# A graph layer on one core: dense edge weights computed by ScalarE in PSUM, and eight groups of edges gathered last

## What is computed

```python
hs, hd = h[src], h[dst]
e = concatenate([hs, hd], axis=1)
a_k = exp(relu(e @ W_att_k + b_att_k))            # k = 1, 2, 3, one number an edge
att_k = segment_sum(a_k, dst)
avg_a = (a_1 / att_1[dst] + a_2 / att_2[dst] + a_3 / att_3[dst]) / 3
m = avg_a * relu(relu(relu(hs @ W1 + b1) @ W2 + b2) @ W3 + b3)
h_neigh = segment_sum(m, dst) / maximum(deg, 1)
out = relu(concatenate([h, h_neigh], axis=1) @ W_c1 + b_c1) @ W_c2 + b_c2
return layernorm(x + out)
```

## Time and profile before

| | us |
|---|---|
| median of three runs (lowest, highest) | 785.11 (784.7, 786.55) |
| the profiled execution | 788.37 |
| its span in the profile | 784.4 |
| busy: TensorE, VectorE, GpSimd, ScalarE | 635.0, 562.6, 573.6, 460.2 |
| mean granted TensorE clock, share of full | 0.858 |

### The profile page before, as it was taken

How to read it: one execution, slowest core, us unless ns; L and a number is a source line. 1 busy time by engine, 2 the same in 40 slices (tenths; PEclk the granted TensorE clock), 3 DMA queues, 4 the chain that set the end, 5 groups by cost and what they waited for, 6 DMA issues and landing times.

```text
span 784.4 us, 17056 instructions
## 1 busy us (share of the span) xinstructions
PE 635.0 (81%) x5157; PEld 519.2 (66%) x5157; DVE 562.6 (72%) x1855; ACT 460.2 (59%) x1109; POOL 573.6 (73%) x604
## 2 busy tenths in 40 slices
PE   9951889988878777999998788797778877878775
PEld 5741657764655456899988677685667766767664
DVE  4884587588888787788886666665567777677566
ACT  6566687578655455667765555553365556566533
POOL 7777777777777677777777777777777777777760
PEclk9985596599778776899999989988798988899698
DMA  7974263334862233333433333324344444444321
GB/s 228 252 195 105 66 101 84 71 85 78 69 83 75 54 96 80 83 87 87 88 83 80 78 74 83 73 64 133 66 107 104 104 111 128 104 117 104 89 59 35
DMA packets 83313, 75.69 MB, mean 96 GB/s; under 512 B 35064, under 2 KB 66720, under 8 KB 83216
## 3 DMA queue, kind: packets, MB, share of 16 engines
q0 software_dynamic: 19008, 39.82, 25.8%
q1 hardware_dynamic: 63920, 34.59, 16.3%
q10 hardware_dynamic: 288, 0.13, 0.1%
HBM read 64.94 MB, written 9.52 MB: 95 GB/s over the span
## 4 chain that ended last, share of the span: by engine, by line
PE 33%; POOL 30%; issue 13%; DVE 11%; ACT 6%; DMA 5%; DVEq 1%; SPq 0%; POOLq 0%; ACTq 0%
POOL work L1247 30%; PE bank L1434 8%; PE bank L1473 7%; PE bank L1457 4%; PE bank L1440 2%; DVE counts L1730 2%; ACT fin L1578 2%; DVE acc L1907 2%; PE bank L592 2%; PE bank L613 2%; PE bank L1391 1%; DVE fin L1717 1%; PE bank L601 1%; DMA message_table<-work 1%; PE bank L1419 1%
## 5 line engine op out<-in xcount | busy, mean ns | idle before, releaser
L1247 POOL DMA_INDIRECT work<-message_table,src_t x554 | 531.6, 960 | 174.2 <-issue 164.9
L1434 PE MATMUL bank<-work 128*128 128x144 f32 (+8 forms) x1188 | 188.5, 314 | 37.9 <-DVE acc L1907 37.8
L1434 PEld LDWEIGHTS bank<-work 128*128 128x128 f32 x1188 | 174.3, 223 | 50.8 <-issue 43.8
L1604 ACT COPY work<-bank 128x192 f32<-128x192 f32 (+7 forms) x126 | 37.4, 297 | 177.4 <-DVE work L1859 176.0
L1473 PE MATMUL bank<-shared,fin 128*128 128x129 f32 (+1 forms) x882 | 115.1, 286 | 0.0
L1907 DVE TENSOR_TENSOR acc<-acc,bank 128x192 f32 (+8 forms) x297 | 89.1, 300 | 27.4 <-issue 3.6
L1473 PEld LDWEIGHTS bank<-shared,fin 128*128 128x128 f32 (+1 forms) x882 | 106.1, 197 | 2.5 <-issue 0.6
L1890 DVE TENSOR_TENSOR work<-bank,work 128x576 f32<-128x576 f32 (+7 forms) x126 | 86.2, 684 | 13.1
L1765 DVE SCALAR_TENSOR_TENSOR fin<-logits_or_x,per_node,counts 128x384 f32<-128x384 f32 (+1 forms) x147 | 85.8, 611 | 1.9 <-PE bank L1473 1.9
L904 PE MATMUL bank<-rest_w,acc 128*128 128x128 f32 x294 | 52.3, 344 | 40.5 <-DVE fin L995 31.0
L904 PEld LDWEIGHTS bank<-rest_w,acc 128*128 128x128 f32 x294 | 46.5, 246 | 43.0 <-DVE fin L995 32.3
(11 more groups left out here) (162 smaller groups left out, 840.4 us busy)
## 6 DMA issues: line engine op xcount, KB each, us to landing
work<-message_table,src_t POOLq DMA_INDIRECT x554
side<-near_nodes SPq DMA_DIRECT2D x102, 48.0 KB
side<-logit_parts SPq DMA_DIRECT2D x297, 0.8 KB
message_table<-work SPq DMA_DIRECT2D x12, 262.0 KB, 4.7
work<-message_table SPq DMA_DIRECT2D x48, 65.5 KB
work<-in_x_t SPq DMA_DIRECT2D x12, 256.0 KB, 4.9
fin<-in_x SPq DMA_DIRECT2D x11, 256.0 KB, 3.0
logits_or_x<-in_x_t SPq DMA_DIRECT2D x11, 256.0 KB, 3.7
```

Source lines behind the costliest of these rows:

```text
L1247: pool.indirect_dma_start(out=rows_of(n)[:, t, :], out_offset=None, in_=table[:, :], in_offset=bass.IndirectOffsetOnAxis(ap=src_t[:, h, g: ...
L1434: pe.matmul(sums[:, at:at + HEADS * w], rows_here[:, t, 0:P], wt_of(i)[:, t, :], start=h == 0, stop=h == TILES - 1)
```

## The change

Dense weights: `scale_rows` goes. ScalarE computes relu(A*B - 1) for a block and a head over 384 destinations into the bank `EXP_BANK` (`hot_excess`), and VectorE's `hot_weights` reads that bank, adds 1 (or 0 where a bound on the logits fails) and multiplies by the counts. TensorE takes the loaded rows unscaled. There is one bank: write `n` waits for weight `n - 1` (`s_hw`), weight `n` for write `n` (`s_hr`). ScalarE's order in a step is write 1, mask copy, exp, one-hots, write 2, write 0 of the next block. SyncE's reload of a block's buffer waits for the block's matmuls instead of its scaling.

Order: groups 100 to 107, whose edges end in node block 3, leave their place among the long units and become four short units at the end. There are 22 long units of four groups and 127 units in all. A bound on their nodes joins the check for the second pass.

Finals: block 3 becomes the last piece, alone. The others are three blocks, ten times four, two, two and one, so there are 15 pieces. `A`, `B` and `C` start nine, six and four steps before the end of the loop, and `final_tail` is written anew.

The diff, cut to its core (left out: assertions, buffer views, the lists of the late rows' transfers):

```diff
@@ -62,6 +62,7 @@
 EARLY_FROM, EARLY_EVERY = 3, 2
+LATE_BLOCK, LATE_FROM, LATE_GROUPS = HOT, 100, 8
@@ -125,13 +126,19 @@
     HOT_AT = COUNT_STEPS + 2
-    LONG = COUNT_STEPS
+    LONG = COUNT_STEPS - 1
     long_from = -(-n_hot // (2 * pair)) * 2 * pair
-    long_end = long_from + (LONG - 1) * 2 * pair
-    assert long_end < n_groups and CELL % (2 * pair) == 0
+    late_a, late_b = LATE_FROM, LATE_FROM + LATE_GROUPS
+    long_end = long_from + (LONG - 1) * 2 * pair + LATE_GROUPS
+    assert long_end < n_groups and CELL % (2 * pair) == 0 == (late_a - long_from) % (2 * pair)
+    assert long_from <= late_a and late_b <= long_end and late_a // CELL == (late_b - 1) // CELL
+    assert LATE_GROUPS % (2 * pair) == 0
     first_order = [tuple(range(n_hot, long_from))]
-    first_order += [tuple(range(g, g + 2 * pair)) for g in range(long_from, long_end, 2 * pair)]
+    first_order += [tuple(range(g, g + 2 * pair)) for g in range(long_from, long_end, 2 * pair)
+                    if not late_a <= g < late_b]
     first_order += [tuple(range(g, min(g + pair, n_groups))) for g in range(long_end, n_groups, pair)]
+    MAIN = len(first_order)
+    first_order += [tuple(range(g, g + pair)) for g in range(late_a, late_b, pair)]
     again_order = [tuple(range(g, min(g + pair, n_groups))) for g in range(0, n_groups, pair)]
@@ -255,8 +262,8 @@
         hot_wt = fin[:, 0:THREE * n_hot_w].rearrange("p (j k d) -> p j k d", j=THREE, k=HEADS)
-        shared = sb("shared", [P, TWO * HEADS * (P + 1)])
-        hot_scaled = shared[:, :].rearrange("p (j k f) -> p j k f", j=TWO, k=HEADS)
+        SHARED = 5 * P
+        shared = sb("shared", [P, SHARED])
         n_out = HOT * HEADS * (P + 1)
@@ -488,6 +495,8 @@
                 dve.memset(one_col[:, :], 1.0)
+                dve.memset(less_one[:, :], -1.0)
+                dve.memset(shared[:, COLS:SHARED], 0.0)
                 dve.memset(eps_col[:, :], EPS / DOWN)
@@ -666,35 +675,38 @@
-        sizes = [CHUNK] * (n_blocks // CHUNK - 1)
-        rest = n_blocks - sum(sizes) - 1
-        sizes += [rest - rest // 2, rest // 2, 1]
-        finals = [(sum(sizes[:c]), nb) for c, nb in enumerate(sizes)]
+        n_four = (n_blocks - LATE_BLOCK - 1) // CHUNK - 1
+        sizes = [LATE_BLOCK] + [CHUNK] * n_four
+        rest = n_blocks - 1 - sum(sizes)
+        sizes += [(rest - 1) // 2, rest // 2, 1]
+        finals = [(sum(sizes[:c]) + (c > 0), nb) for c, nb in enumerate(sizes)] + [(LATE_BLOCK, 1)]
         FINAL_EVERY, FINAL_STEPS = (4, 3), 8
         A, B, C = LAST - 3, LAST - 2, LAST - 1
+        assert sorted(i for b, nb in finals for i in range(b, b + nb)) == list(range(n_blocks))
         assert finals[LAST][1] == 1 and finals[B][1] <= LAST_FROM and finals[C][1] <= LAST_FROM
             most = share * n_edges + 6 * math.sqrt(share * (1 - share) * n_edges)
-            return min(len(first_order) - 1, sum(u[-1] < int(most / GROUP) for u in first_order))
+            return min(MAIN - 1, sum(u[-1] < int(most / GROUP) for u in first_order[:MAIN]))
             final_at.append(max(at_least, expected_end(c) + 2))
-        final_at += [expected_end(A) + 1, expected_end(B) + 1]
-        assert final_at[A - 1] + 3 <= final_at[A] == U - 9 and final_at[B] == U - 5 and expected_end(C) <= U - 3
-        ready = [at - 2 for at in final_at[:A]] + [expected_end(A), expected_end(B), expected_end(C), U - 1]
+        final_at += [U - 9, U - 6, U - 4]
+        assert final_at[A - 1] + 3 <= final_at[A] and U - 4 == MAIN
+        assert all(expected_end(c) < final_at[c] for c in (A, B, C))
+        ready = [at - 2 for at in final_at[:A]] + [at - 1 for at in final_at[A:]] + [U - 1]
         final_tail = {
-            U - 4: [(B, 1), (A, 5)],
-            U - 3: [(B, 2), (A, 6)],
-            U - 2: [(B, 3), (A, 7)],
-            U - 1: [(C, 0), (B, 4), (LAST, 0), (LAST, 1), (C, 1), (LAST, 2), (B, 5), (C, 2), (LAST, 3), (LAST, 4),
-                    (C, 3), (LAST, 5), (B, 6), (C, 4), (B, 7), (C, 5), (LAST, 6), (C, 6), (LAST, 7), (C, 7)],
+            U - 4: [(B, 2), (A, 5), (C, 0), (C, 1)],
+            U - 3: [(B, 3), (C, 2), (A, 6), (B, 4), (B, 5), (B, 6)],
+            U - 2: [(C, 3), (A, 7), (B, 7), (C, 4)],
+            U - 1: [(LAST, 0), (LAST, 1), (C, 5), (LAST, 2), (C, 6), (LAST, 3), (C, 7), (LAST, 4), (LAST, 5), (LAST, 6),
+                    (LAST, 7)],
         }
...
@@ -730,10 +742,12 @@
             for g in u:
-                node_limits[g] = least_node(i)
+                node_limits[g] = least_node(i) if i < MAIN else LATE_BLOCK * P
         limit_runs = [(a, len(list(run))) for a, run in itertools.groupby(node_limits)]
-        limit = mask[0:1, 1:THREE, :].rearrange("p j c -> p (j c)")[:, 0:n_groups]
-        assert n_groups <= (THREE - 1) * columns_most
+        n_limits = n_groups + LATE_GROUPS
+        limits = mask[0:1, 1:THREE, :].rearrange("p j c -> p (j c)")[:, 0:n_limits]
+        limit, late_limit = limits[:, 0:n_groups], limits[:, n_groups:n_limits]
+        assert n_limits <= (THREE - 1) * columns_most
@@ -1275,7 +1295,7 @@
                         if b >= BLOCKS:
-                            sp.wait_ge(s_hr, HEADS * (b - BLOCKS + 1))
+                            sp.wait_ge(s_hm, b - BLOCKS + 1)
                         m = block_nodes(b)
@@ -1466,14 +1486,14 @@
                                           zero_col[:, 0:1].to_broadcast([P, HEADS * (P + 1)]), start=True, stop=False)
-                        pe.wait_ge(s_hr, HEADS * (b + 1))
+                        rows_here = hot_block[0:m, b % BLOCKS, 0:1 + P]
+                        pe.wait_ge(s_hb[b % BLOCKS], 16 * (b // BLOCKS + 1))
                         for k in range(HEADS):
                                                  hot_wt[0:m, b % THREE, k, h * P:(h + 1) * P],
-                                                 hot_scaled[0:m, b % TWO, k, :],
-                                                 start=False, stop=b == n_blocks - 1 and k == HEADS - 1)
+                                                 rows_here, start=False, stop=b == n_blocks - 1 and k == HEADS - 1)
                         last.then_inc(s_hm, 1)
@@ -1530,18 +1550,17 @@
-                    def scale_rows(b):
-
-                        m = block_nodes(b)
-                        if b == 0:
+                    def hot_excess(b, k):
+
+                        m, n = block_nodes(b), HEADS * b + k
+                        if n == 0:
+                            act.wait_ge(s_hl, 16 * (HEADS * HOT + 1))
+                            act.wait_ge(s_cadd, n_hot)
                             act.wait_ge(s_ok, OK_STEPS)
-                            act.wait_ge(s_e3, EARLY)
-                        act.wait_ge(s_hb[b % BLOCKS], 16 * (b // BLOCKS + 1))
-                        if b >= TWO:
-                            act.wait_ge(s_hm, b - TWO + 1)
-                        for k in range(HEADS):
-                            act.activation(hot_scaled[0:m, b % TWO, k, :], hot_block[0:m, b % BLOCKS, 0:1 + P], ACT.Copy,
-                                           scale=powers[0:m, b, k:k + 1]).then_inc(s_hr, 1)
+                        else:
+                            act.wait_ge(s_hw, n)
+                        act.activation(bank[EXP_BANK][0:m, 0:hot_nodes], hot_b[0:m, k, :], ACT.Relu, bias=less_one[0:m, 0:1],
+                                       scale=powers[0:m, b, k:k + 1]).then_inc(s_hr, 1)
@@ -1632,6 +1651,8 @@
                     for i in range(n_steps):
+                        if first and 0 <= i - HOT_AT - 1 < n_blocks:
+                            hot_excess(i - HOT_AT - 1, 1)
                         if i + 1 < n_units:
@@ -1656,7 +1677,9 @@
                         if first and 0 <= i - HOT_AT - 1 < n_blocks:
-                            scale_rows(i - HOT_AT - 1)
+                            hot_excess(i - HOT_AT - 1, 2)
+                        if first and 0 <= i - HOT_AT < n_blocks:
+                            hot_excess(i - HOT_AT, 0)
@@ -1684,7 +1707,10 @@
                                                 ALU.is_lt))
-                        chain(dve.tensor_reduce(late[:, :], limit[0:1, :], AX, ALU.max))
+                        most_late = float((LATE_BLOCK + 1) * P - width_of(late_a))
+                        chain(dve.tensor_scalar(late_limit[0:1, :], bank[SIDE_BANKS[0]][0:1, late_a:late_b], most_late, None,
+                                                ALU.is_gt))
+                        chain(dve.tensor_reduce(late[:, :], limits[0:1, :], AX, ALU.max))
                     dve.wait_ge(s_fill, 1)
@@ -1756,14 +1782,11 @@
                         m = block_nodes(b)
-                        if b == 0 and k == 0:
-                            dve.wait_ge(s_hl, 16 * (HEADS * HOT + 1))
-                            dve.wait_ge(s_cadd, n_hot)
-                            dve.wait_ge(s_ok, OK_STEPS)
+                        dve.wait_ge(s_hr, HEADS * b + k + 1)
                         if b >= THREE:
```

(5 more changed lines are left out.)

33 lines of the change are left out of this document (19 added, 14 removed).

## The result

The changed kernel takes 813.94 us, median of six runs (811.19 to 819.67), against 783.71 us (781.25 to 786.55) of the kernel before in the same comparison: a ratio of 1.0394, interval 1.035 to 1.0437, or 30.2 us more. The forecast was 795 us in a range of 781 to 808. The direction was right, the size was not: 20.6 us are missing from a sum that came to +9.6.

A forecast was written before the change was run, and what follows sets the result against it. Gathers were taken to set the pace before, and the consumers after the change. Terms +6.2 (dense), +2.7 (unit), -2.3 (narrower units), +6 (finals) and -3 (tail) gave +9.6 on 785.1: 795 us, range 781 to 808.

The forecast's parts named there:

- The turn on the bank: Dense stage: ScalarE and VectorE alternate on one PSUM bank three times a block; mean step 5.18 us, stage 40.0 us longer.
- The lag isn't worked off to the end: After the dense stage: of its 40.0 us, +6.2 stays after later gather waits absorb what they can.
- the pace of units with finals: While finals run, a unit costs 4.57 us without gather waits, so a lead is worked off at only 0.4 us a unit.
- Of the 40.0 the later waits for gathers absorb at most their 33.8: Behind the dense stage: VectorE's 33.8 us of gather waits taken off the 40.0 us of longer stage.
- left: What remains of the dense stage's 40.0 us after the later gather waits absorb their share: +6.2 us.
- (4) Tail [...] -3: Behind the last addition: block 3 alone as last piece, 10.9 us instead of 13.6; with a narrower last unit, -3.
- Unit, finals and block 3: One more unit +2.7 us, narrower last units -2.3, finals +6 for three more blocks inside the loop and one more piece.
- Gathers the bound: Rival: gathers stay the bound, the lead being worked off before the last unit; 781 us, chance 0.17.
- partly: Rival: the lead is partly worked off, at 0.58 to 0.63 us a write; 782 to 790 us, chance 0.15.
- Ring full: Rival: steps over 5.45 us fill the 48-tile ring, so gathering stops too; 808 us, chance 0.08.
- The late block doesn't pay: Rival at the end: block 3's finals only replace the last blocks', losing the 3 us; 798 us, within the forecast's 0.60.

The follow-up runs named there:

- Kernel 3: The changed kernel with ScalarE's excess written to three SBUF buffers instead of the one PSUM bank, same instruction order: 784.53 us, ratio 1.0017.
- kernels 3 and 6: 6: dense change with three SBUF buffers, a block's three writes together a step ahead: 783.85 us in the old order, 787.15 us in the new.
- Kernel 1: The kernel before with only the dense weights changed; order, finals and end list as before: 800.19 us, ratio 1.0215.
- three lags: Units 30 to 77 longer by 28.0, 43.6 and 58.7 us: kernel before plus two zero matmuls a dense block, dense change alone, kernel before plus three.
- the pair with three matmuls: Three zero-adding matmuls per dense block but the last, added to the kernel before (816.86 us) and to the kernel with the new order alone (829.59 us).
- the old list: The whole change with the old end list: pieces B and C stay out of the last units and run behind the last unit; 803.84 us, ratio 1.0258.
- kernel 2: The kernel before with only the order, the finals' pieces and the end list changed; dense weights as before: 789.05 us, ratio 1.0088.
- two matmuls: The kernel before with two zero-adding matmuls added to each dense block but the last: 789.97 us, ratio 1.0106.

## Why the prediction was right and wrong

**The turn on the bank: right.** 675 ns for a write of 0.67 forecast, 614 for a weight of 0.61, 5.19 us for a step of 5.17 to 5.18. The stage grew by 41.7 us (252.2 less 210.5) where +40.0 was forecast, by 43.2 in the dense change alone. Kernel 3 shows that the turn is the cause. The prediction's case for 0.61 proved less than it said: it drew its 1.05 ns a column through the bank's 344 ns and SBUF's 611 ns, and then found the two on one line. A slope from other rows would have carried it, since L1890, which reads a bank, takes 608 ns for 432 columns and 758 for 576, 1.04 a column. A weight that reads the bank takes 614 ns, one from SBUF 611, and the same instruction in kernels 3 and 6, from SBUF, 613 and 611. The Trainium skill ("VectorE: DVE Perf Modes", section on the TRN2 errata) has 62 cycles more for PSUM, an estimated 0.065 us; the trace doesn't agree, the difference is 3 ns.

**The lag isn't worked off to the end: right,** and the pace of units with finals too. Kernel 1 took 170.0 us for 37 units from unit 80 to the ninth last, 4.59 us each; the forecast was 4.57. The changed kernel took 179.8 us for 38, 4.73 each.

**"Of the 40.0 the later waits for gathers absorb at most their 33.8": the first step that failed.** The bound was taken as the value. Over three lags the later stages gave back 21.8, 27.1 and 26.1 us. By stretch, the waits of before behind the dense stage are 6.1 us up to unit 80, 19.2 to the ninth last and 8.5 in the last eight (33.8 in all); kernel 1 recovered 7.2, 14.7 and 5.1. A wait for gathers had covered others that came out when it went: behind the dense stage VectorE waited 7.1 us for TensorE's logits (3.3 before) and 14.8 for ScalarE's exps (13.2 before), and TensorE's own waits for VectorE stayed. So the term "left" was 43.6 - 27.1 = 16.5 and not 6.2: 10.3 of the missing 20.6 us, some 3 in the stage and 7 in what was absorbed.

**"(4) Tail [...] -3": the second.** The tail did shrink, by 2.3 us in the traces. But the sum counted only what lies behind the last addition. The steps of `B` and `C` that left the tail had gone into the last units, at places where nothing covers them, and those units were priced by their narrower columns alone (-2.3). For last units and tail together the sum thus has -5.3 where the traces have +2.8 against the dense change alone, and +1.7 in the pair with three matmuls. With the old list the whole change costs 10.1 us less by the medians (the two ratios, 1.0394 and 1.0258 with their intervals, leave 6 to 15); the two traces place 7.1 us of it in the last eight units, less the 2.6 us of tail, 4.5 in all. The other 5.6 us I could not place: the two kernels were not timed together, from unit 29 to the ninth last their stages differ by 2.9 us the other way, and 10.3 of the 11.9 us between their spans lie before unit 29's sums, which the list doesn't touch.

**Unit, finals and block 3: of the right size.** Forecast +2.7 and +6 less 2.3, together 6.4 without the tail. The whole change with the old list less the dense change alone: 3.6 us by the medians. The traces have 9.7 us more in the second column of the changed kernel than in the dense change alone, against the +2.7 and +6.

**The step from 6.4 and -3 to 13.7.** By the medians: 16.5 for the turn, 3.6 for unit, pieces and block, 10.1 for the list: 30.2. That it adds up is no check, since each term is the difference of two of these medians. The traces give the list 4.5 and leave the more to unit and pieces. Both have the end as a loss where the forecast had a gain; how the 13.7 divide isn't shown closer than that.

**The rivals.** *Gathers the bound* and *partly* are out: no wait for gathers is left, and the last unit lies 38 us behind the last gather. *Ring full* came at the edge (GpSimd waited 12.7 us for TensorE's L1460, in 19 waits, against 7.4 in 11 before) and cost nothing. *The late block doesn't pay* was the right side and too mild: the new order as a whole costs 0.8 to 5.3 us without a lag (kernels 2, 3 and 6) and about 13 with one.

**Not settled:** why two matmuls cost 6.2 us although the last unit is summed 8.5 us after the last gather's start again, as before (the last gather started 447.5 us after unit 29 instead of 439.4; 554 gathers of 967 ns instead of 960 would be 4 of these 8); why the new order costs 5.3 us in kernel 2 and 0.8 in kernel 3; how the 13.7 us divide between the list and the unit and pieces; and whether the old list would bring the new order to the time of before without a lag, for which no undisturbed run is there.

## What to carry to other kernels

A single buffer between two engines makes their times add: here 0.67 and 0.61 us three times a step, 42 us over 49 steps; three buffers made the same arithmetic free (+0.8 us for the whole change with them, interval -0.7 to +3.3). Slack read off as "waits for X" is an upper bound of what a delay can hide, since waits on other engines lie beneath it: here 22 to 27 of 33.8 us were given back, in three kernels. Expect every item that was free under it to be charged once it is used up. And a shorter tail is a gain only if the work taken out of it is covered where it goes; price the units that take it over, with each handoff of the moved steps in line, and look at the granted clock of the stretch that the price is read from.

## What the runs showed of the hardware

ScalarE writes 384 columns with scale and bias from columns in 675 ns to PSUM and 692 ns to SBUF. VectorE's weight takes 614 ns with one operand in PSUM, and 611 to 613 with all in SBUF. Eight matmuls of 60 columns take 1.80 us at a granted clock of 0.50, and eight of 108 columns 1.11 us at 1.00.

On two chips every kernel took 1002 to 1020 us instead of 784 to 814, mostly with engines idle for longer. TensorE was slower too: in kernel 1 its granted clock was 0.78 instead of 0.88, and a dense matmul took 318 ns instead of 291; VectorE's and ScalarE's instructions took what they take elsewhere (weight 614, write 675 ns). GpSimd's gathers in kernel 1 there:

```profile
L1249 POOL DMA_INDIRECT work<-message_table,src_t x554 | 526.6, 951 | 342.0 <-issue 149.4 <-remote 102.6 <-PE bank L1442 82.0
```

The gathers take the same 951 ns as on the other chip; 342 us of idle time stand before them instead of 169.2. Of these, 82.0 are waits for a slot that TensorE hasn't freed (3.1 there) and 102.6 are put down to "remote", a cause outside the program's own waits that nothing here explains. Differences of 3% between kernels vanished there, so a comparison is worth only as much as the time of the kernel before on the same chip.
